# A fused decoder layer: the geometric scores and the q/k transposes of one batch element moved to the head of the next turn, on PE, ACT and DVE

## What is computed

```python
# attention, 8 query heads on 2 key heads, 32 wide; per batch element
q, k, v = norm(x) @ Wq, norm(x) @ Wk, norm(x) @ Wv
q, k = rope(q), rope(k)
out = softmax(causal(q k^T / sqrt(32))) @ v
qp, kp = q[..., :3] . dirs[h], k[..., :3] . dirs[h]      # one number per token and head
geo_out = softmax(causal(qp[t] * kp[s])) @ v             # the geometric product
x = x + (out + scales[h] * (geo_out - out)) @ Wo
# context: a decayed running sum over tokens (WKV), keys = norm(x), values = ctx
# feed-forward: Hadamard transform, 8-bit activations, ternary weights, silu(gate) * up, down
```

## Time and profile before

| what | value |
|---|---|
| median of 3 runs | 450.31 us (449.54 to 451.16) |
| the profiled execution, its own time | 450.48 us |
| its span, first to last instruction | 448.7 us |
| PE busy | 368.2 us, 82% of the span |
| PE weight loads busy | 253.9 us, 57% |
| DVE busy | 355.1 us, 79% |
| ACT busy | 269.5 us, 60% |
| POOL busy | 110.0 us, 25% |
| granted TensorE clock, mean | 0.953 of full speed |

### The profile page before, as it was taken

How to read it: one execution, slowest core, us unless ns; L and a number is a source line. 1 busy time by engine, 2 the same in 40 slices (tenths; PEclk the granted TensorE clock), 3 DMA queues, 4 the chain that set the end, 5 groups by cost and what they waited for, 6 DMA issues and landing times. The chain is left out here.

```text
span 448.7 us, 7687 instructions
## 1 busy us (share of the span) xinstructions
PE 368.2 (82%) x2354; PEld 253.9 (57%) x2354; DVE 355.1 (79%) x936; ACT 269.5 (60%) x534; POOL 110.0 (25%) x160
## 2 busy tenths in 40 slices
PE   2988878898788878887888876597888999989794
PEld 1754554555455545454545444375767777777573
DVE  4586878988899889888986567888979889897642
ACT  1254566566766676657675555668748585675542
POOL 1210312220222022202230123432333333232210
PEclk9988999999999999999998588798999999999899
DMA  7960012000000000000000000000000000000001
GB/s 217 292 203 0 2 31 88 12 1 15 12 13 1 13 12 14 2 11 15 12 6 7 13 1 0 1 2 0 1 24 11 15 14 12 25 2 23 12 25 36
DMA packets 13711, 13.43 MB, mean 30 GB/s; under 512 B 2007, under 2 KB 12887, under 8 KB 13543
## 3 DMA queue, kind: packets, MB, share of 16 engines
q1 hardware_dynamic: 13671, 12.94, 9.8%
HBM read 10.84 MB, written 2.10 MB: 29 GB/s over the span
## 5 line engine op out<-in xcount | busy, mean ns | idle before, releaser
L695 PE MATMUL wide<-had,c_h_hi 128*128 128x512 f32 x128 | 55.8, 436 | 8.6 <-ACT c_q2T L475 8.1
L412 POOL TENSOR_TENSOR c_h_lo<-c_hb,c_h_hi 128x512 fp32r<-128x512 f32 x32 | 40.8, 1273 | 74.6 <-ACT c_h_hi L464 69.3
L695 PE MATMUL wide<-had,c_h_lo 128*128 128x512 f32 x128 | 53.2, 415 | 0.0
L680 PE MATMUL wide<-c_q_T,w_tern_all 128*128 128x256 bf16 x256 | 36.5, 283 | 7.6 <-DVE c_hh L1029 6.0
L457 ACT ACTIVATE c_sl<-c_z 128x512 f32<-128x512 f32 x32 | 20.1, 629 | 31.6 <-DVE c_z L1020 31.4
L906 PE MATMUL bank<-w_o,a_att 128*128 128x256 f32 x128 | 32.9, 401 | 2.9 <-DVE a_att L1191 2.2
L695 PEld LDWEIGHTS wide<-had,c_h_hi 128*128 128x128 f32 x128 | 25.5, 199 | 15.8 <-issue 10.8
L680 PEld LDWEIGHTS wide<-c_q_T,w_tern_all 128*128 128x128 bf16 x256 | 23.6, 101 | 18.3 <-DVE c_hh L1029 8.1
L378 POOL TENSOR_TENSOR a_qk<-a_rot_c,a_rot_s 128x320 f32<-128x320 f32 x16 | 13.8, 865 | 71.7 <-DVE a_rot_s L1162 71.7
L1029 DVE TENSOR_TENSOR c_hh<-wide,c_sl 128x512 f32<-128x512 f32 x32 | 22.1, 691 | 10.2 <-ACT c_sl L457 10.2
L906 PEld LDWEIGHTS bank<-w_o,a_att 128*128 128x128 f32 x128 | 23.9, 196 | 11.0 <-DVE a_att L1191 7.2
(11 more groups left out here) (188 smaller groups left out, 1007.6 us busy)
## 6 DMA issues: line engine op xcount, KB each, us to landing
x_res<-in_x SPq DMA_DIRECT2D x4, 512.0 KB, 7.5
b_vT<-in_ctxT SPq DMA_DIRECT2D x16, 128.0 KB, 2.2
out<-c_yo SPq DMA_DIRECT2D x16, 128.0 KB, 1.7
w_raw_all<-in_wg SPq DMA_DIRECT2D x1, 1024.0 KB, 8.7
w_raw_all<-in_wu SPq DMA_DIRECT2D x1, 1024.0 KB, 10.8
w_raw_all<-in_wd SPq DMA_DIRECT2D x1, 1024.0 KB, 13.2
had_f<-in_h SPq DMA_DIRECT2D x1, 1024.0 KB, 4.8
w_o_raw<-in_Wo SPq DMA_DIRECT2D x4, 128.0 KB, 6.7
```

The costliest lines, as they stand in the source:

```text
L412: nc.gpsimd.tensor_tensor(h_lo[p][:, j::FQ, :], hb[j % 2][:, :].rearrange("c (m t) -> c m t", m=2), h_hi[p][:, j::FQ, :].bitcast(F32), ALU ...
L680: mm = nc.tensor.matmul(dst[:, m * TOK:(m + 1) * TOK], w[:, k * FF + blk * P:k * FF + blk * P + P], q_T[p][:, k * TOK:(k + 1) * TOK], star ...
L695: mm = nc.tensor.matmul(wide[:, 1 + i, m * 512:(m + 1) * 512], a[p][:, j + FQ * m, i * P:(i + 1) * P], had512[:, j, :], start=(j == 0 and ...
```

## The change

Apart from a few semaphore waits that come in and the eight idle matmuls of the first full product, which go, no instruction is added or taken away; every engine's stream has a new order. Line numbers here are those of the changed kernel.

- The q/k transposes of an element stand at the head of the following turn (stage m), and their copy a_qkT is the first thing that ACT does in it.
- The geometric product of an element stands at the head of the following turn (now stage b), behind the transposed tile, and its exponential behind the copy a_xT. For the last element both stay at the end of their turn.
- The projection stands ahead of the row transposes; the transposed scores behind the weighted values; the keys behind the transposed scores.
- ACT does the logarithm and reciprocal of d ahead of those of b, and both ahead of the q/k split of f; the exponential a_e_s comes behind the split; the ternary weights (`ternary`) ahead of the row copies.
- DVE begins a turn with the two scans, then b_xn, a_mx, b_dnm and b_num, the rotation, then the row work; the split, a_att and b_y come ahead of a_g_diag.

```diff
@@ PE
+                def geometric(u, p):
+                    need(pe, A["eg"], u)
+                    need(pe, B["en"], KC * (u - 1))
...
                 def body(f, m, b, c, d):
+                    if m is not None and m[0] == NB - 1:
+                        turn_x(0, 0)
+                    if m is not None:
+                        u, p = m
...
+                        need(pe, A["hi"], 2 * (u + 1))
+                        need(pe, A["lo"], 2 * (u + 1))
+                        need(pe, A["mx"], u)
+                        need(pe, A["stk"], u)
+                        for j, sp in enumerate([split_q[p]] * 4 + [split_k[p]] * 4):
+                            mm = nc.tensor.transpose(scores[:, j * P:j * P + P].bitcast(F32R),
+                                                     sp[:, (j % 4) * P:(j % 4) * P + P], ident_r[:, :])
+                        mm.then_inc(A["tq"], 1)
+                    if f is not None:
+                        u, p = f
+                        need(pe, A["xn"], u + 1)
+                        need(pe, A["att"], u - 2)
+                        for k in range(KC):
+                            mm = nc.tensor.transpose(turn[:, k * P:k * P + P], xn[p][:, k * P:k * P + P], ident[:, :])
+                        mm.then_inc(A["t1"], 1)
+                    if b is not None and b[0] < NB - 1:
+                        geometric(*b)
...
-                    if c is not None and m is not None:
-                        keys(*c)
-                    if m is not None:
-                        u, p = m
-                        need(pe, A["mrow"], 2 * (u + 1))
...
+                    if m is not None:
+                        u, p = m
+
+                        need(pe, A["es"], u)
+                        for half in range(2):
+                            nc.tensor.matmul(scoresT[:, half * 512:half * 512 + 512], ident_b[:, :], mask_st[:, :],
+                                             start=True, stop=True)
...
+                        mm.then_inc(A["sT"], 1)
+                    if c is not None and m is not None:
+                        keys(*c)
                     if c is not None and m is None:
                         keys(*c)
                     if m is not None:
                         u, p = m
...
+                        need(pe, A["sT"], u + 1)
+                        need(pe, A["mrow"], 2 * (u + 1))
@@ ACT
+                def geometric_weights(u, p):
+                    need(act, A["geo"], u + 1)
+                    need(act, A["pn"], u - 1)
+                    nc.scalar.activation(e_g[p][:, :], geo[:, :], ACT.Exp).then_inc(A["eg"], 1)
+
                 def body(f, m, b, c, d):
+                    if m is not None:
+                        u, p = m
+                        need(act, A["tq"], u + 1)
+                        need(act, A["nm"], u - 1)
+                        nc.scalar.copy(qkT[p][:, :], scores[:, :]).then_inc(A["qT"], 1)
...
+                    if b is not None and b[0] < NB - 1:
+                        geometric_weights(*b)
+                    if m is not None and m[0] >= 4:
+                        ternary(m[0] - 4)
```

More of the change, by code:

```diff
@@ L564, in body @@
                         nc.scalar.activation(e_s[p][:, :], scoresT[:, :], ACT.Exp, scale=SCALE).then_inc(A["es"], 1)
[L565 to L575, removed]
-                    if m is not None:
-                        u, p = m
[L578 to L588, removed]
+                    if m is not None and m[0] == NB - 1:
+                        geometric_weights(*m)
                     if f is not None:
                         u, p = f
-                        need(act, A["tq"], u + 1)
-                        need(act, A["nm"], u - 1)
-                        nc.scalar.copy(qkT[p][:, :], scores[:, :]).then_inc(A["qT"], 1)
                         need(act, A["dir"], u + 1)
@@ L796, in body @@
                         u, p = f
[L797 to L832, removed]
                         if u == 0:
@@ L884, in body @@
                         u, p = m
[L885 to L889, removed]
-                        if u == 0:
-                            idle_work(turn, 8)
-                        need(pe, A["stk"], u + 1)
-                        need(pe, A["gd"], u + 1)
-                        for g in range(2):
-                            mm = nc.tensor.matmul(geo[:, g * 512:g * 512 + 512], stack[p][:, 1, :],
-                                                  g_diag[p][:, g * 512:g * 512 + 512], start=False, stop=True,
+                        need(pe, A["sT"], u + 1)
+                        need(pe, A["mrow"], 2 * (u + 1))
+                        for h in range(H):
+                            mm = nc.tensor.matmul(scoresT[:, h * P:h * P + P], pick_neg[:, h * P:h * P + P],
+                                                  m_row[p][:, :], start=False, stop=True,
                                                   skip_group_check=True)
-                        mm.then_inc(A["geo"], 1)
+                        mm.then_inc(A["nm"], 1)
+                    if m is not None and m[0] == NB - 1:
+                        geometric(*m)
                     if b is not None:
@@ L1169, in body @@
                         u, p = m
+                        need(dve, A["grow"], u + 1)
+                        need(dve, A["gm"], u - 1)
+                        nc.vector.tensor_tensor_scan(cmax[p][:, :], k_row[p][:, :], k_row[p][:, :],
+                                                     k_row[p][:, 0:1], ALU.max, ALU.max).then_inc(A["cmx"], 1)
+                        need(dve, A["mrow"], 2 * u + 1)
+                        nc.vector.tensor_tensor(m_row[p][32:40, :], row_sb[p][0:8, 0:P], m_row[p][0:8, :].bitcast(F32),
+                                                ALU.subtract).then_inc(A["mrow"], 1)
+                    if m is not None:
+                        u, p = m
                         need(dve, A["cmx"], u + 1)
```

151 lines of the change are left out of this document (87 added, 64 removed).

## The result

The changed kernel takes 526.57 us (median of 4 runs, 522.54 to 530.78), the kernel before 449.93 beside it (449.13 to 451.16, 4 runs): ratio 1.167, 95% interval 1.160 to 1.174. The forecast was 529.

A forecast was written before the change was run, and what follows sets the result against it. The bound was taken as a 14.69 us circle: DVE's 8.5 us plus 6.2 us of hand-over through PE and ACT. Forecast: 450.5 + 47 (waits) + 24 (clock) + 9 (head) - 1 (tail) = 529 us, range 499 to 550.

The forecast's parts named there:

- Terms 1 to 3: Full turn up to ACT's exponentials: PE projection through a_v_in 3.3, weighted values 2.2, transposed scores 1.2, keys 0.5 us.
- Terms 1 and 3: PE projection, row transposes and ACT copies through a_v_in, 3.3 us; transposed scores 1.2 and keys 0.5 us.
- term 2: PE's weighted values, waiting for a_v_in and lasting until the masks: 2.2 us.
- Term 4: ACT's stream behind the keys: exponentials 1.0, b_ln and b_inv 0.85, a_lnd and a_inv 1.3, split 0.7 us.
- Terms 5 to 7: DVE rest parts 0.7, a_att 0.75; PE projection 1.65, b_y's transpose 0.3, q/k transposes 1.0; copy and scores 2.75, overrun 0.35 us.
- The clock: PE's 4.2 us idle before the output projection lowers the clock: 2.0 us a turn, 24 over twelve turns.
- Head: First three turns slower as scores and a_qkT wait behind other work: +9 us, bounds 4 and 14.
- Tail: Turn 16, without f, where the weighted values need no a_v_in: -1 us, bounds -4 and +3.
- Rival 1: Keys not late at ACT's exponentials: circle 13.6 us, 440 us, or 436 with POOL's products moved away; chance 0.04.
- Rival 2: The waits come but the clock is kept in the full turns: 505 us; chance 0.14.
- Rival 3: Clock low to the end of the scores in every turn: 548 us; chance 0.16.

The follow-up runs named there:

- Experiments 1 to 3: Changed kernel, keys early: 445.36 us; changed kernel, keys late, ACT's reciprocal of b and split before exponentials: 464.9 us; kernel before, keys late alone: 517.66 us.
- experiment 7: Changed kernel with early keys and ACT's order reciprocal of d, split, reciprocal of b, exponentials on the keys last: 438.59 us, ratio 0.978.
- experiment 1: Changed kernel with the keys' transposes right behind the row transposes on PE, ahead of the weighted values: 445.36 us, ratio 0.993.
- experiment 6: Changed kernel with early keys and ACT's split right behind the exponentials, then reciprocal of b, then of d: 436.76 us, ratio 0.975.
- the repeat of experiment 6: Same kernel (early keys, split right behind the exponentials), no filler, run again in another session: 436.66 us, ratio 0.973.
- the first filler: Changed kernel with 28 idle 128-column matmuls in PE's gap before the output projection, full turns: 523.16 us, ratio 1.168.

## Why the prediction was right

The direction and both causes held. That 529 came so near to 526.6 is in part luck: inside a turn the waits were put too high (3.9 us against 3.0) and the clock too low (2.0 against 2.75), and the two errors cancel. Point by point, zero at the start of the maxima, 174.37:

- **Terms 1 to 3** put ACT's exponentials at 7.2 us; they began at 6.96. Terms 1 and 3 were too long by 0.2 each (a_v_in ended at 3.11, from the masks to the exponentials it took 1.45), term 2 too short by 0.2 (2.40).
- **Term 4** had the split ready at 11.05; DVE's L1210 began at 10.63. Experiments 1 to 3 show that this is the cause: take away the late keys and all of the time is back, take away what stands behind them on ACT and most of it is.
- **Terms 5 to 7** without the clock had 18.55 for the turn. The kernel with 14 idle matmuls, where the clock is kept, has 17.69. Besides the 0.4 above, the extension of the copy by tile and geometric product (0.35) did not show: copy to maxima was 2.77 there. So the waits cost 3.0 a turn, not 3.9. By the maxima of that run (71.59 to 289.71, 218.1 us against 177.4) twelve turns are +40.7, not 47.
- **The clock** was put at 2.0 a turn; it is 2.75 (20.44 - 17.69), and 26.7 over the twelve turns against 24. The term that was mis-sized is the output projection's 0.9. From the start of the projection to that of b_y's transpose it is 3.58 us at the low clock (186.42 to 190.00) and 1.83 at the full one (138.53 to 140.36), so its price is 1.75. From there to the copy a_qkT the low clock costs 0.59 (forecast for 6.5 us of low clock: 0.85), and from the copy to the next maxima 0.41 (forecast: 0.6). The length was too short as well: the recorded text took a value between 3.3 and 6.5 us of low clock, and it was 6.8. Nor do its counts follow from its two rows, since 2.70 - 1.99 is 0.71 and not 0.9, and at that ratio the q/k transposes would lose 0.4 and not 0.65. Above all the row was only in part at the low level. The kernel before, over that row:

```profile
278.38:281.10 2.72, 2.72 (x11) 2.19 (x11) 1.36 (x3) 1.25 (x2) 1.35 (x2) 0.70 0.00 0
```

A clock of 0.70 on average, so 2.70 was a mixture. At 0.50 throughout eight matmuls of the same size take 3.78 us. What was guessed right is what the stretch covers: the projection, b_y's transpose and the q/k transposes, but not the scores. The rule quoted from the Trainium skill, "TensorE: Matmul & The Clock Gate", Part 1, that activity releases the clock, is borne out: 14 idle matmuls gave 25 us.
- **Head:** +8.9 against +9, and near its parts: the second and third maxima are 4.8 us late, where turns 1 and 2 had 4, and turn 3 adds 4.1, where it had 5. **Tail:** -0.2 against -1.
- **Rival 1** was right on the circle (13.6; the runs with the keys early have 13.71 and 13.36) and wrong on the wait. Its lower figure, 436, rested on what POOL's products would give back. The Trainium skill, "GPSIMD Engine Reference", section 1, has POOL contend with VectorE's instructions that have two SBUF inputs, and experiment 7 agrees (0.28 against 0.67 and 0.71 for two such passes). But it gave nothing, since the products then stretch two other passes of that kind, b_y and a_g_diag.
- **Rival 2** (505) is what the 14 idle matmuls make of the kernel: 501. Rival 3 did not come: over the scores the clock is 1.00.

## What to carry to other kernels

Before an instruction is moved down one engine's stream, read who waits for it and what stands behind that waiting instruction in its own in-order stream: here two 128-column transposes, 0.4 us of work a turn, cost 69 us, the clock included, because ACT had a reciprocal and a split queued behind its wait. A gap that such a wait opens on PE has a second price, the clock of the work behind it, and a few idle matmuls that end before the work is ready show how much it is. A price at the low clock must be taken from a row whose own stretch shows 0.50 throughout.

## What was not expected of the hardware

- The low clock costs more than the rows before had shown: 3.78 us for eight 256-column matmuls against 1.99, behind a gap of 4.09 us.
- Smaller gaps can do it too, but not each time. In experiment 1 PE sat idle for 0.84 us ahead of the row transposes at 139.22 and for 1.40 us ahead of the weighted values at 141.46, and the clock was low in what followed. A single gap of this kind never did this: in experiments 1, 6, 7 and the repeat of 6 there are 48 gaps of 1.10 to 1.47 us ahead of the weighted values without another in front of them, and behind each the clock was 1.00 for the next 3 us. But the pair does not decide it either. Each of these four traces has two such pairs, and only in two of the eight did the clock fall, here and at 197.46 in the repeat of experiment 6 (0.96 and 1.31 us, then 0.50). In experiment 1 itself 0.97 and 1.40 us, ending at 198.77, left it at 1.00. What decides is open. The first case:

```profile
141.00:144.00 3.00, 2.54 (x16) 0.73 (x16) 2.80 (x7) 2.43 (x9) 2.17 (x3) 0.61 0.00 0
```

- An idle 128-column f32 matmul shows as two rows of the record and takes 0.24 us (3.39 us for 14), so the first filler was twice as long as planned.
